# Sixteen graphs through two graph networks on one core: exponentials of the first network on ScalarE ahead of the turn, masks in two parts, one more feed-forward piece ahead

## The reference, cut to what matters

```python
# first network, for l in range(3)
scores = si[:, :, None] + sj[:, None, :] + attn_b[l]      # si, sj = x @ attn_w
scores = jnp.where(scores >= 0, scores, 0.2 * scores)
scores = jnp.where(mask, scores, -jnp.inf)                # mask = adjacency + eye > 0
attn = jax.nn.softmax(scores, axis=-1)
h = layernorm(x + attn @ x, g1[l], beta1[l])
ff = gelu(h @ W1[l] + b1[l]) @ W2[l] + b2[l]              # 256 -> 1024 -> 256
x = layernorm(h + ff, g2[l], beta2[l])
...
# second network, 8 heads of 32 features
scores = leaky_relu(a_src[..., :, None] + a_dst[..., None, :] + b_att)
att = jax.nn.softmax(jnp.where(A > 0, scores, NEG_INF), axis=-1)
out = jax.nn.relu(att @ xh)
...
x = layernorm(x + L0(x)); x = layernorm(x + L1(x))
```

## Time and profile before

| what | value |
|---|---|
| median of 3 runs | 2327.34 us |
| the profiled execution | 2329.5 us |
| its span, first to last instruction | 2327.7 us |
| mean granted TensorE clock | 0.984 |
| TensorE busy | 2187.7 us, 94% |
| VectorE busy | 1863.9 us, 80% |
| ScalarE busy | 1636.4 us, 70% |
| GpSimd busy | 201.8 us, 9% |

### The profile page before, as it was taken

One profiled execution on the slowest core, in us unless ns is written; L12 is line 12 of the kernel. 1 busy time (PEld: TensorE's weight loads), 2 busy tenths in 40 slices (PEclk: granted clock), 3 DMA queues, 4 the chain that ended last, 5 costly groups with the idle time before them and its releaser, 6 DMA issues.

```text
span 2327.7 us, 31621 instructions
## 1 busy us (share of the span) xinstructions
PE 2187.7 (94%) x10117; PEld 1525.1 (66%) x10117; DVE 1863.9 (80%) x5743; ACT 1636.4 (70%) x3151; POOL 201.8 (9%) x200
## 2 busy tenths in 40 slices
PE   5999998999999999999999999999999999999766
PEld 3766666676667667667766766676676667667453
DVE  5566587688888888888888888888888888877867
ACT  2344467777787777778777777777777777778676
POOL 0000100010101001010100101010010101001000
PEclk9999999999999999999999999999999999999888
DMA  6011133227455362735436274553627455364201
GB/s 219 1 36 55 47 108 127 86 87 236 131 179 157 114 213 86 245 122 186 150 123 206 85 241 125 178 158 114 212 86 229 138 171 165 97 202 153 92 28 37
DMA packets 162145, 315.74 MB, mean 136 GB/s; under 512 B 10392, under 2 KB 82620, under 8 KB 153532
## 3 DMA queue, kind: packets, MB, share of 16 engines
q1 hardware_dynamic: 161980, 313.72, 42.5%
HBM read 235.82 MB, written 77.86 MB: 135 GB/s over the span
## 4 chain that ended last, share of the span: by engine, by line
PE 71%; DVE 20%; ACT 5%; issue 2%; POOL 1%; DMA 1%; DVEq 0%; SPq 0%; POOLq 0%; ACTq 0%
PE ffn L1341 19%; PE av L1258 14%; PE av L1330 10%; PE ffn L1330 10%; PE pT L1240 7%; PE av L1282 4%; DVE prob L846 3%; DVE prob L837 2%; DVE stats L778 2%; PE av L1317 1%; DVE lone L806 1%; PE av L1365 1%; PE trow L1365 1%; DVE xs L972 1%; DVE xs L966 1%
## 5 line engine op out<-in xcount | busy, mean ns | idle before, releaser
L1341 PE MATMUL ffn<-w_sb,G 128*128 128x256 f32 x3072 | 724.1, 381 | 12.5 <-ACT G L560 12.5
L1341 PEld LDWEIGHTS ffn<-w_sb,G 128*128 128x128 f32 x3072 | 571.1, 191 | 94.1 <-ACT G L560 18.1
L846 DVE CUSTOM_DVE_ANT_0 prob<-trow,mask 128x512 f32<-128x512 f32 x676 | 438.5, 686 | 31.7 <-PE trow L1219 19.6
L1330 PE MATMUL ffn<-hT,w_sb 128*128 128x512 f32 x768 | 364.0, 601 | 4.4 <-DVE xs L959 1.3
L1330 PE MATMUL av<-hT,w_sb 128*128 128x512 f32 x768 | 358.2, 596 | 0.0
L500 POOL TENSOR_TENSOR rstd<-veps,mhalf 128x4 f32<-128x4 f32 x127 | 170.5, 1342 | 2087.4 <-DVE veps L774 2087.4
L536 ACT ACTIVATE prob<-prob,s 128x512 f32<-128x512 f32 x484 | 329.4, 715 | 7.7 <-DVE aw_row L853 4.3
L542 ACT ACTIVATE prob<-prob,nm 128x512 f32<-128x512 f32 x464 | 329.2, 714 | 0.0
L1240 PEld LDWEIGHTS pT<-ident,prob 128*128 128x128 f32 x1648 | 208.2, 144 | 134.0 <-issue 103.3
L1240 PE MATMUL pT<-ident,prob 128*128 128x128 f32 x1648 | 251.3, 278 | 27.2 <-DVE prob L908 14.6
L1330 PEld LDWEIGHTS ffn<-hT,w_sb 128*128 128x128 f32 x768 | 140.1, 191 | 152.2 <-issue 134.1
(11 more groups left out here) (164 smaller groups left out, 2739.5 us busy)
## 6 DMA issues: line engine op xcount, KB each, us to landing
w_sb<-in_L_gnn_W SPq DMA_DIRECT2D x92, 1024.0 KB, 8.8
blocks_dram<-blocks SPq DMA_DIRECT2D x264, 256.0 KB, 4.2
prob<-blocks_dram SPq DMA_DIRECT2D x66, 1024.0 KB, 4.9
trow<-rows_dram SPq DMA_DIRECT2D x127, 256.0 KB, 3.7
adj_sb<-in_adj SPq DMA_DIRECT2D x16, 1024.0 KB, 9.0
xin<-in_x SPq DMA_DIRECT2D x16, 512.0 KB, 6.0
x0r<-in_x SPq DMA_DIRECT2D x16, 512.0 KB, 10.0
out<-o SPq DMA_DIRECT2D x15, 512.0 KB, 6.9
```

What stands on the lines that cost most here:

```text
L846: return v.tensor_tensor_reduce(out=out_[:, t, :], in0=targets, in1=mask[:, t, :], scale=1.0, scalar=LEAST, op0=ALU.add, op1=ALU.max, accu ...
L1330: last = te.matmul(ff1[f % len(ff1)][:], w1_sb[:, weights_of(g) % STAGES, dt, f * P:(f + 1) * P], hT[:, dt, :], start=dt == 0, stop=dt == ...
L1341: last = te.matmul(ffn[part][:, at:at + D], G[:, f, t * P:(t + 1) * P], w2_sb[:, weights_of(g) % STAGES, f, :], start=f == 0, stop=f == FT ...
```

## The change

1. ScalarE adds `nm0` and takes the exponential of the first network in one instruction, in `prob0`, ahead of the turn (`first_exponential`); after the turn it only copies the bank out (`probabilities`). VectorE's `first_exponents` is gone. Two of the four `score0` of a unit now stand behind the last gelu, and the other heads' scores and exponentials follow the four copies instead of standing between them.
2. The normalisation of a finished graph (`graph_out`) goes from VectorE to ScalarE (`normalise(LAST, ...)`), with `nmean` and `shift` for it.
3. `make_masks` becomes `mask_edges` and `mask_diagonal`. In kind-0 units the edges stand ahead of `attention`; `find_lone` goes from the kind-0 unit to the kind-2 unit before it.
4. The block turns are placed anew: head 2 of a graph is turned behind `attention` in its kind-0 unit (before: in the kind-1 unit), head 4 ahead of `attention` in the kind-1 unit (before: at its end). Heads 1, 6 and 7 stay.
5. `spent_behind` becomes 1 in every unit.
6. One more piece of the second product stands ahead of `attention`, one fewer behind.

```diff
 def turned_ahead(g):
-    return [q for q in turned(g) if moved(q)][:1] if g % 3 != 1 else []
+    return [q for q in turned(g) if moved(q)][:1] if g > min(FIRST_MADE) + 1 else []
 def turned_behind(g):
-    if g % 3 == 1:
-        return [q for q in turned(g - 1) + turned(g) if moved(q)][-2:] if g > 1 else []
-    return [q for q in turned(g) if moved(q)][1:] if g % 3 == 2 else []
+    return [q for q in turned(g) if moved(q)][len(turned_ahead(g)):]
 def spent_behind(g):
-    return 3 if g % 3 == 0 else 1
+    return 4 if g % 3 == 0 and HEADS - 3 in BY_BLOCKS else 1
+def masked(g):
+    return g // 3 + 1 if g > 3 and g % 3 == 0 and g // 3 + 1 < GRAPHS else None
...
+            def first_exponential(t):
+                act.wait_ge(s_score0, c("score0"))
+                nc.scalar.activation(prob0[:, t, :], prob0[:, t, :], ACT.Exp, bias=nm0[:, t:t + 1], scale=1.0).then_inc(s_arg, 1)
             def probabilities(t):
                 act.wait_ge(s_pt, c("pt"))
-                nc.scalar.activation(prob0[:, t, :], pT[t % BANKS][:], ACT.Exp).then_inc(s_prob, 1)
+                nc.scalar.copy(prob0[:, t, :], pT[t % BANKS][:]).then_inc(s_prob, 1)
+            def first_network_probabilities(u, scored):
+                first_exponential(0)
+                for t in range(1, T):
+                    if t >= scored:
+                        score0(u, t)
+                    first_exponential(t)
+                    probabilities(t - 1)
+                probabilities(T - 1)
...
-                    if f >= FT - 2:
-                        score0(g + 1, 2 * (f - FT + 2))
-                        score0(g + 1, 2 * (f - FT + 2) + 1)
-                for t in range(T):
-                    probabilities(t)
+                    if f == FT - 2:
+                        score0(g + 1, 0)
+                        score0(g + 1, 1)
+                first_network_probabilities(g + 1, 2)
+                for t in range(T):
                     for q in held[:1]:
                         exponential(q, t)
...
+                if leaving(g) is not None:
+                    normalise(LAST, o1, o1, s_out)
...
-            def first_exponents(t):
-                dve.wait_ge(s_score0, c("score0"))
-                v.tensor_scalar(prob0[:, t, :], prob0[:, t, :], nm0[:, t:t + 1], None, ALU.add).then_inc(s_arg, 1)
...
                 for q in turned_ahead(g):
                     turn_blocks(q)
+                if masked(g) is not None:
+                    mask_edges(masked(g) % 2)
                 attention(graph2, l2, *new[1:2])
                 for q in turned_behind(g)[:1]:
                     turn_blocks(q)
                 if done is not None:
                     graph_sum(done)
                 plus_bias(graph, l)
                 fed_forward(graph, 0)
-                if leaving(g) is not None:
-                    graph_out()
...
                 elif g > 3 and g % 3 == 2:
                     keep_masks(g // 3 % 2)
-                elif g > 3 and g % 3 == 0 and g // 3 + 1 < GRAPHS:
-                    find_lone((g // 3 + 1) % 2)
-                    make_masks((g // 3 + 1) % 2)
+                    if g // 3 + 2 < GRAPHS:
+                        find_lone(g // 3 % 2)
+                elif masked(g) is not None:
+                    mask_diagonal(masked(g) % 2)
...
-                ahead, inside, behind = (4, (1, 1), (1, 1, 1, 1)) if four is None else (2, (2, 1), (2, 1, 2, 1))
+                ahead, inside, behind = (5, (1, 1), (1, 1, 1, 0)) if four is None else (3, (2, 1), (2, 1, 1, 1))
```

More of the change, by code:

```diff
@@ L52 @@
 OWN_PLACE = (LAST_HEADS - SIDE, LAST_HEADS - SIDE + 1)
-ATTENDED, RESIDUAL, FED, LAST = range(4)
+ATTENDED, RESIDUAL, LAST, FED = range(4)
 COLS = LAYERS * (2 * DT + FT)
@@ L289, in build @@
         s_av1, s_oT, s_back, s_av1e = sem("av1"), sem("oT"), sem("back"), sem("av1e")
-        s_ve, s_rstd, s_shift = sem("ve"), sem("rstd"), [sem("shift0"), sem("shift1")]
+        s_ve, s_rstd, s_shift = sem("ve"), sem("rstd"), [sem(f"shift{i}") for i in range(3)]
         s_hn, s_hT, s_hTe, s_ff1, s_gelu = sem("hn"), sem("hT"), sem("hTe"), sem("ff1"), sem("gelu")
@@ L678, in _ @@
                 gelu(1, f)
-                if f >= T:
+                if f >= T and not moved(first - 2):
                     turned_out(first - 2, f - T)
@@ L702, in _ @@
                 score0(UNITS - 2, t)
-            for t in range(T):
-                probabilities(t)
+            first_network_probabilities(UNITS - 2, T)
             for t in range(T):
@@ L780, in statistics, with block, mask_edges @@
                 aggregate(which)
-            def make_masks(s):
-                def block(m, t):
-                    return m[:, t, t * P:(t + 1) * P]
+            def block(m, t):
+                return m[:, t, t * P:(t + 1) * P]
+            def mask_edges(s):
                 v.tensor_scalar(mask0[s][:], adj_sb[:], 0.0, -BIG, ALU.is_le, ALU.mult).then_inc(s_dch, 1)
@@ L1067, in _ @@
             find_lone(0)
-            make_masks(0)
+            mask_edges(0)
+            mask_diagonal(0)
             dve.wait_ge(s_aw, 32)
@@ L1071, in _ @@
             first_targets(0)
-            for t in range(T):
-                first_exponents(t)
             dve.wait_ge(s_const, 16 * CONSTS)
@@ L1147, in _ @@
             plus_bias(GRAPHS - 1, 1)
-            turn_blocks(first - 3)
+            for q in turned_ahead(REGULAR):
+                turn_blocks(q)
             head_made(second)
             fed_forward(GRAPHS - 1, 0)
-            turn_blocks(first - 1)
+            for q in turned_behind(REGULAR):
+                turn_blocks(q)
             head_made(third)
@@ L1268, in attend_heads @@
             def attend_heads(q):
-                by_act, by_vector = all_out[[h for h in range(q, q + SIDE) if not moved(h)][-1], T - 1]
-                pe.wait_ge(s_prob, by_act)
-                if by_vector:
-                    pe.wait_ge(s_copy, by_vector)
+                by_engine = [h for h in range(q, q + SIDE) if not moved(h)]
+                if by_engine:
+                    by_act, by_vector = all_out[by_engine[-1], T - 1]
+                    pe.wait_ge(s_prob, by_act)
+                    if by_vector:
+                        pe.wait_ge(s_copy, by_vector)
                 if any(moved(q + i) for i in range(SIDE)):
@@ L1417, in _ @@
                         for q in heads[:1]:
-                            turn(q, f - T)
+                            if not moved(q):
+                                turn(q, f - T)
                 pieces(ahead)
```

31 lines of the change are left out of this document (17 added, 14 removed).

## The result

The changed kernel takes 2434.61 us (median of 4 runs, 2433.86 to 2436.98) against 2327.95 us (2326.52 to 2328.57) for the kernel before on the same chip: ratio 1.0461, 95% interval 1.0443 to 1.0479. It is 107 us slower; the forecast was slower by 62, within 2345 to 2410, so the direction was right and the size outside the range. The profiled span grew from 2327.7 to 2432.1 us.

What follows compares the result with a forecast made beforehand. TensorE, busy 94%, was taken as the bound, with VectorE and ScalarE meeting it at fixed places. The terms 48 + 3 + 19 - 9 + 5 - 5 + 5 + 4 - 6 = +64 us gave 2391, stated as 2390, range 2345 to 2410.

Steps and rivals of the forecast that it cites:

- Head sums of kind-0 units: TensorE, moved earlier by spent_behind 3 to 1, waits 4.0 us for head 7's load in 12 units: +48.
- The piece ahead: In units 0 to 5, one piece fewer behind attention lengthens each wait for the state by 0.86 us: +5.
- Exponentials ahead of the turn: ScalarE's exponentials make the first turn 0.2 us late in 24 units: +5; VectorE's relief is worth nothing by itself.
- `fed_forward` 0: Head 2's turn ahead of it in kind-0 units delays the next first product 0, +1.45 us in 13 units: +19.
- `find_lone`: In kind-2 units it delays the next scores; 3.1 us hidden under the head sums' wait, alone only in unit 9: +3.
- Kind 1, -5: Gelu perhaps 0.6 us sooner, piece shortens the exponential's wait, against 2.5 us more ScalarE work: -5, out of -20 to +12.
- Kind 2, -9: With head 2 turned outside kind-1 units, the waits at the kind-2 head sums go: -9.
- The start, +12: Early units: piece in units 0 to 5 +5, ScalarE-bound units and first attention +4, find_lone in unit 9 +3.
- The end, -6: VectorE's 8.06 us wait for stores near the end goes; last exponentials ahead of the turn cost 1 us: -6.
- rivals with a late head in time or no change: Head sums cost nothing: 2307, chance 0.11; or head-sum wait stays and other waits vanish: 2330, chance 0.04.
- Only half of it: Rival: kind-0 head-sum wait falls to find_lone's 3.1 us and fed_forward 0 is met in time: 2361, chance 0.15.
- rival with ScalarE as the bound: ScalarE, carrying 117 us more, becomes the bound in kinds 1 and 2, 1 us in 28 units: 2418, chance 0.08.

Runs made afterwards that it cites:

- b2: Kernel before with only the head sums of kind-0 units moved behind first product 1: 2381.83 us, ratio 1.0228.
- e4: Changed kernel with 32 useless transposes filling the wait ahead of the head sums of kind-0 units from unit 12 on: 2418.97 us.
- b3: Kernel before with only one more piece of the second product ahead of attention and one fewer behind: 2362.31 us, ratio 1.0142.
- e6: e3 with the pieces of the second product as in the kernel before: 2388.91 us, ratio to the kernel before 1.0248.
- b1: Kernel before with only the first network's exponentials on ScalarE ahead of the turn, VectorE's additions gone: 2392.81 us, ratio 1.0269.
- e3: Changed kernel with head sums of kind-0 units back behind first product 3 and find_lone back in kind-0 units: 2383.42 us.
- e1: Changed kernel with only the head sums of kind-0 units back behind first product 3: 2411.6 us, ratio to the kernel before 1.0356.
- e2: Changed kernel with only find_lone back in kind-0 units: 2442.78 us, ratio to the kernel before 1.0486.
- x2: Kernel before with all four ramps of kind-1 units behind the last gelu on ScalarE: 2314.3 us, ratio 0.9939.
- e7: e3 with no ramp ahead of the last gelu in kind-1 units: 2370.0 us, ratio to the kernel before 1.0178.
- x1: Kernel before with the head sums of kind-2 units put behind first product 2: 2318.59 us, ratio 0.9958.
- b4: Kernel before with only graph_out moved to ScalarE: 2331.6 us, ratio 1.0003.
- b6: Kernel before with block turns and mask edges placed anew, find_lone staying, head 2 of kind-0 units turned behind fed_forward 0: 2358.31 us, ratio 1.0116.

## Why the prediction was right and wrong

The terms of the forecast sum to +64, and the medians differ by +107. Two things were put at nothing and cost most: what a wait does to the clock, and what the piece ahead takes from the turn of the state and the projection.

- **Head sums of kind-0 units: right in place and chain, 42 for 48.** The load's issue and the landing stand where they were forecast; the wait is 3.5 us, not 4.0. TensorE came 0.4 us later than I had it, the state's turn having waited ahead. b2 shows the step alone.
- **What that wait does to the clock: a term that is missing, 19 us.** I priced a stall at its own length. With the fall to 1.2 GHz behind it each costs 1.7 us more, 19 us in 11 units by the rows, 16 by e4.
- **The piece ahead: the step that failed, 18 us for 0.** I counted the piece at the head sums, the target row and first product 0, and at the state only in units 0 to 5 (+5). For the later units I left the state out. There the waits at the turn of the state and the projection grew by 18 us between 500 and 2200 (12.7 + 8.4 - 2.7), and alone the piece costs 33 (b3). In kind-0 units show why: 0.25 us of wait at the turn of the state, so no slack (0.24 and 0.86 are the 1.10 of b3). In the changed kernel the block turn beside it hides most of that (0.35, and as much in kind 2). The largest part, 1.06 us at the projection of kind-1 units, stands where no row shows a wait; without the piece it is 0.20 (e6). What the piece gave back I had counted, as the 0.86 us that shorten the wait for the first exponential.
- **Exponentials ahead of the turn: mis-sized.** 0.39 us in kinds 2 and 0 instead of 0.2 in 24 units, and 0.52 in kind 1. I took the table load to start where the ramp had been, and the ramp had started 0.11 us before the end of the copy ahead of it; the load starts behind that end. Set against the 9.5 us of first exponentials that go, it is +6, near the +5. But alone it is the dearest part (b1, +63): my sum had it cheap because the piece in front hides 0.86 us of each wait, and I did not charge the price of that. Exponentials and piece, with the turns and `graph_out` that take 5 off (e6 less b1), are +55 together (e3).
- **`fed_forward` 0: right.** 15.6 us, 1.3 in 12 units, for 19 and 1.45 in 13.
- **`find_lone`: right in being hidden, wrong in place.** Under the head sums' wait it is hidden; with that wait gone it costs 28 us (e1 less e3) for the forecast 12 x 3.1 = 37, and it is met at first product 3. Back in kind 0 alone (e2) it costs 8 more, of which 6 are the gelu's waits of kind 1.
- **Kind 1, -5: right in size.** The gelu's waits fell by 6.4 us, 0.5 a unit for my 0.6. VectorE is earlier there because `find_lone` left kind 0 (e2 and e3, with it back, have 10.6), and what passes this on to the gelu is the ramps' place (x2, e7), which I had not seen.
- **Kind 2, -9:** right, no waits at head sums are left there. x1 gets the same by one first product and pays nothing.
- **The start, +12 for 19:** both the piece (b3) and the exponentials (b1) cost 11 to 15 us there alone, up to unit 9. By the trace of the changed kernel 11 us are waits and up to 8.5 clock, again a term that I did not have.
- **The end, -6: failed.** VectorE's wait for the stores is gone as forecast, but it waits 8.85 us for TensorE's pieces instead, and the end gained nothing.

```profile
2251.30 0.69 DVE L978 TENSOR_TENSOR xs<-ffn,xs 128x512 f32<-128x512 f32 x1 [8.85 <-PE ffn L1361]
```

- **`graph_out` at 0: right** (b4, +1.0, interval over zero).

The forecast terms for the stretch from unit 10 on came to 58 us (48 - 9 + 19 + 5 - 5) and it lost 85. The runs also divide the change in two. For `spent_behind` and `find_lone` together I had 48 + 3 = 51 us, and they cost 52 (changed kernel less e3); that is in part luck, for 19 us of clock that I did not have stand against waits that are shorter than forecast (39.5 more at the head sums for 48) and 6 that the gelu's fell by. For all the rest (e3) I had 13, and it cost 55: the miss lies there, in the piece, the start and the end.

The rivals with a late head in time or no change were out. "Only half of it" needed a head sums' wait of 3.1 us and `fed_forward` 0 in time; the wait was 3.5, and `fed_forward` 0 was late. The rival with ScalarE as the bound gave 2418 and was nearest in size. TensorE does wait for ScalarE at the state, 21 us in 36 units, but b3 has as much with no work added to ScalarE, and e6, with the work and without the piece, has 2.4: it is the piece that makes these waits and not ScalarE's load. (Two of the rivals' sums are off by a little: 2327 + 37 - 32 is 2332, not 2330, and 2327 + 64 + 28 is 2419.)

What stays open: why the head sums at 1321.31, behind a wait of 3.40 us, kept their clock when 11 others did not, and 6 of 11 waits of 2.1 to 2.4 us in e1 passed without a fall; and where the other 7 us went that b6 saved in waits.

## What to carry to other kernels

A stage moved ahead of a meeting point is taken from behind another: name both, and look for the slack at each in every kind of unit, not only where the trace already shows a wait. Where there is already a wait of 0.2 us there is no slack, and what is taken there next costs in full (0.24 became 1.10 in b3). Where an engine idles for an input while work that is ready stands behind it in its own order, swap the two first: that gave 15 us here (x2) with no work saved, and moving 93 us of additions off VectorE lost 63 (b1).

## What the runs showed of the hardware

A single wait of TensorE of 3.3 to 3.7 us, once in some 140 us, halved its clock for 3.4 us of the work behind it in 11 cases of 12, where in the kernel before it stood at 2.4 GHz throughout this stretch. Shorter waits can do it too: in b1 it fell in 5 kind-1 units of 12, behind 0.90 and then 1.38 us, and in e1 behind 5 of 11 waits of 2.1 to 2.4 us. There first product 3 took 1.98 us in one unit and 3.24 in another behind the same wait:

```profile
1451.46 1.98 PE L1350 MATMUL ffn<-hT,w_sb 128*128 128x512 f32 x4 [2.12 <-DVE xs L978]
1592.63 3.24 PE L1350 MATMUL ffn<-hT,w_sb 128*128 128x512 f32 x4 [2.12 <-DVE xs L978]
```

And a 128x4 instruction of GpSimd takes 1.26 instead of 0.20 us beside a VectorE instruction with two inputs in SBUF, which a placement that only looks at VectorE's own time does not see.
